# Shorter norm chains in three stages and an earlier choice of experts in a twelve-stage kernel

## What is computed

```python
# stage 1 (L0_attn): two norms in a row, then linear attention and an MLP
x = x + _L0_attn_ref(_layernorm(x), ...)      # in it: xn = _rmsnorm(x, scale1)
# stage 10 (L3_attn): retention, a norm per head, a gate
var = jnp.mean(o * o, axis=-1, keepdims=True)
o = o * jax.lax.rsqrt(var + EPS) * gnorm_w
o = o * (g * jax.nn.sigmoid(g))
return o.reshape(B, T, H * HEAD_V) @ Wo.T
# stage 11 (L3_ffn), called with _layernorm(x)
h = _layer_norm(x, ln1_g, ln1_b)
h = _self_attention(h, wq, bq, wk, bk, wv, bv, wo, bo)
x = x + h
h = _layer_norm(x, ln2_g, ln2_b)
# _moe_ffn(h): 512 tokens, 8 experts, capacity C = 128
logits = x @ wr
probs = jax.nn.softmax(logits, axis=-1)
top1 = jnp.argmax(probs, axis=-1)
m1 = jax.nn.one_hot(top1, N_EXPERTS, dtype=x.dtype)
top2 = jnp.argmax(jnp.where(m1 > 0, -jnp.inf, logits), axis=-1)
loc1 = jnp.cumsum(m1, axis=0) - 1.0
loc2 = jnp.cumsum(m2, axis=0) - 1.0 + m1.sum(0, keepdims=True)
# tokens with loc < C go to their experts' buffers; the two outputs
# are added with the renormalized probabilities as weights
```

## Time and profile before

| | |
|---|---|
| runs | 1654.95, 1656.37, 1659.03 us; median 1656.37 |
| the profiled execution: time, span | 1656.19 us, 1654.4 us |
| mean granted clock of TensorE | 0.961 |
| PE busy | 1525.7 us, 92% |
| DVE busy | 799.6 us, 48% |
| ACT busy | 621.1 us, 38% |
| POOL busy | 145.1 us, 9% |

### The profile page before, as it was taken

One profiled execution on the slowest core, in us unless ns is written; L12 is line 12 of the kernel. 1 busy time (PEld: TensorE's weight loads), 2 busy tenths in 40 slices (PEclk: granted clock), 3 DMA queues, 4 the chain that ended last, 5 costly groups with the idle time before them and its releaser, 6 DMA issues.

```text
span 1654.4 us, 23522 instructions
## 1 busy us (share of the span) xinstructions
PE 1525.7 (92%) x9628; PEld 934.4 (56%) x9628; DVE 799.6 (48%) x1418; ACT 621.1 (38%) x1161; POOL 145.1 (9%) x185
## 2 busy tenths in 40 slices
PE   7999899999999999999989899999999989677798
PEld 3667544445667554667555455555555555444697
DVE  5553530003433433332452577788889844665432
ACT  1212421011433322433521357677777782104111
POOL 0001120000000301000110312202200000000000
PEclk9999999999999999999999999999999999678699
DMA  9024133200024301022141476454956205100050
GB/s 374 30 102 165 62 110 102 74 28 27 0 102 155 121 0 34 1 102 111 35 136 80 83 144 115 99 93 86 213 84 163 37 2 217 51 1 1 1 204 13
DMA packets 40402, 147.08 MB, mean 89 GB/s; under 512 B 6092, under 2 KB 21708, under 8 KB 30668
## 3 DMA queue, kind: packets, MB, share of 16 engines
q1 hardware_dynamic: 40296, 145.58, 31.0%
HBM read 122.99 MB, written 22.56 MB: 88 GB/s over the span
## 4 chain that ended last, share of the span: by engine, by line
PE 85%; DVE 9%; ACT 4%; issue 2%; DMA 0%; SPq 0%; DVEq 0%; ACTq 0%
PE PS L156 54%; PE PS L1818 8%; PE PS L1735 7%; PE PS L1720 4%; PE PS L565 3%; PE PS L1194 2%; DVE SM L1834 1%; PE PS L1371 1%; PE PS L1204 1%; ACT CN L1417 1%; PE PS L2287 1%; PE PS L2223 1%; DVE SM L2319 1%; ACT L260 1%; PE PS L1809 1%
## 5 line engine op out<-in xcount | busy, mean ns | idle before, releaser
L1834 DVE TENSOR_REDUCE SM<-PS 128x1 f32<-128x1024 f32 x256 | 303.6, 1219 | 66.6 <-PE PS L1720 64.5
L156 PE MATMUL PS<-CT,HT 128*128 128x512 f32 x416 | 190.4, 593 | 2.0 <-ACT HT L669 2.0
L156 PE MATMUL PS<-CN,AR 128*128 128x256 f32 (+1 forms) x832 | 188.0, 371 | 0.0
L156 PEld LDWEIGHTS PS<-CN,AR 128*128 128x128 f32 x832 | 151.2, 190 | 43.9 <-issue 28.7
L156 PE MATMUL PS<-HT,AR 128*128 128x512 f32 x328 | 160.1, 641 | 15.7 <-ACT HT L330 10.4
L1735 PE MATMUL PS<-AR 49*128 49x256 bf16 (+1 forms) x1216 | 162.8, 272 | 1.1 <-DVE AR L1855 0.7
L156 PE MATMUL PS<-AR 128*128 128x512 f32 (+3 forms) x472 | 145.8, 463 | 7.0 <-DVE AR L600 2.5
L1735 PE MATMUL PS<-AR,CT 49*128 49x256 bf16 (+1 forms) x832 | 124.9, 273 | 0.6 <-DVE SM L1878 0.5
L156 PEld LDWEIGHTS PS<-AR 128*128 128x128 f32 x472 | 83.7, 192 | 69.3 <-issue 51.8
L156 PEld LDWEIGHTS PS<-HT,AR 128*128 128x128 f32 x328 | 64.8, 205 | 102.0 <-issue 99.1
L156 PEld LDWEIGHTS PS<-CT,HT 128*128 128x128 f32 x416 | 73.7, 190 | 70.9 <-issue 66.0
(11 more groups left out here) (305 smaller groups left out, 2020.0 us busy)
## 6 DMA issues: line engine op xcount, KB each, us to landing
CN<-ctx_n SPq DMA_DIRECT2D x24, 1024.0 KB, 4.8
AR<-k_parts SPq DMA_DIRECT2D x114, 128.0 KB
CT<-pack SPq DMA_DIRECT2D x7, 2048.0 KB, 7.5
k_parts<-CN SPq DMA_DIRECT2D x32, 384.0 KB, 3.7
CT<-k_parts SPq DMA_DIRECT2D x78, 128.0 KB
CN<-v_ones SPq DMA_DIRECT2D x8, 1152.0 KB, 8.9
CT<-ctx_t SPq DMA_DIRECT2D x8, 1024.0 KB, 19.0
AR<-pack SPq DMA_DIRECT2D x16, 512.0 KB, 3.9
```

The costliest lines, as they stand in the source:

```text
L156: last = te.matmul(o, l, r, start=first and k == 0, stop=final and k == n - 1, skip_group_check=True)
L1834: ve.tensor_reduce(MX9[:, p % 2, e, g % 8 // 4, g % 4:g % 4 + 1], PS[:, b:b + 2, :].rearrange("p a b -> p (a b)"), AX, ALU.max).then_inc(* ...
```

## The change

Names in the rows below: L is the line in the kernel that the row is of (the new kernel's lines are shifted).

Stage 1. Z is made from X in one norm: since the variance of H is v / (v + eps), the two scales together are 1 / sqrt(256 v), with the factor 16 staying where it was. Z, its turns and HT come first; H is made after them, for POOL only. The squares, their sums and one of the chains are gone.

```diff
-        def norm_dve(dv, s, src, dst, mv, rs, *points, name="h"):
+        def norm_dve(dv, s, src, dst, mv, rs, *points, name="h", scale=1.0, eps=1e-5):
             ve = dv.e
             dv.wait_ge(*points)
-            ve.tensor_scalar(rs, mv[:, :, 1], 1.0, 1e-5, ALU.mult, ALU.add).then_inc(*dv.inc("norm", name + "_var", s))
+            ve.tensor_scalar(rs, mv[:, :, 1], scale, eps, ALU.mult, ALU.add).then_inc(*dv.inc("norm", name + "_var", s))
...
-            norm_dve(dv, 1, X, H, xmv, s1_rs[0], *x_norm(1))
-            rms_dve(dv, 1, "z", H, Z1, s1_ss[0], s1_rs[1])
+
+            norm_dve(dv, 1, X, Z1, xmv, s1_rs[1], *x_norm(1), name="z", scale=256.0, eps=0.0)
...
             scaled("zt", W1["s1"])
+            norm_dve(dv, 1, X, H, xmv, s1_rs[0])
...
-            begin_act(ac, 1, s1_rs[0])
-            rms_act(ac, 1, "z", H, Y1, s1_ss[0], s1_rs[1], *[[p] for p in h_all(1)])
+            begin_act(ac, 1, s1_rs[1], "z")
+            norm_act(ac, 1, s1_rs[0])
...
+            out_row(0)
+            out_row(1)
+            out_row(2)
+            inverse(0)
+            out_row(3)
+            inverse(1)
+            gated(0)
+            inverse(2)
+            gated(1)
+            inverse(3)
+            gated(2)
+            gated(3)
+            turned_out_10(dv, 0)
...
+            def root(i):
+                ac.wait_ge(("o_inv", i))
+                ae.activation(rr10[:, i, :], rr10[:, i, :], ACT.Sqrt).then_inc(*ac.inc("root", "o_rs", i))
+
             for i in range(4):
                 for h in range(4):
                     ac.wait_ge(("oo", i), ("rot", 3), ("osq", i - 1, 3) if i else None)
                     ae.activation((tA, tB)[i % 2][:, tok(h)], OO[:, i, tok(h)], ACT.Square,
                                   accum_out=ss10[:, i, h:h + 1]).then_inc(*ac.inc("square", "osq", i, h))
-                ac.wait_ge(("o_inv", i))
-                ae.activation(rr10[:, i, :], rr10[:, i, :], ACT.Sqrt).then_inc(*ac.inc("root", "o_rs", i))
+                if i:
+                    root(i - 1)
+            root(3)
+            turned_out_10(ac, 1)
...
+                pl.wait_ge(("g", 10, i), ("w", 10))
+                pl.wait_last()
+                pl.e.tensor_tensor(g, g, W10["gn"].unsqueeze(1).to_broadcast([128, 4, 128]), ALU.mult).then_inc(
+                    *pl.inc("row", "gn", i))
...
+        M12 = AR[:, o + 1664:o + 1696].bitcast(BF16).rearrange("p (a b) -> p a b", b=8)
+        TRIU11, ONES11 = AR[:, o + 1696:o + 1760].bitcast(BF16), AR[:, o + 1760:o + 1824].bitcast(BF16)
+        oh11, oh11b = M12[:, 0:4, :], M12[:, 4:8, :]
...
             yield "dispatch", 0
+            yield "weights", 0
             for e in range(8):
                 yield "hidden", e
-                if e:
+                if e == 0:
+                    yield "rows", 0
+                    yield "gates", 0
+                else:
                     yield "combine", e - 1
                 if e + 1 < 8:
                     yield "dispatch", e + 1
+                    yield "gates", e + 1
                 yield "result", e
...
-            pe.wait_ge(*before, ("m1", 11), ("m2", 11))
-            te.matmul(blocks, CS["triu"], M12, start=True, stop=False, skip_group_check=True)
+            pe.wait_ge(*before, ("oh", 11), ("oh2", 11), ("counts", 11))
+            te.matmul(blocks, TRIU11, M12, start=True, stop=False, skip_group_check=True)
             for n in range(7):
                 first = n + 1 if n < 3 else 4 if n == 3 else n + 1
                 row = M12[:, n:n + 1, :].to_broadcast([128, 8 - first, 8])
-                z = te.matmul(blocks[:, first:8, :], CS["ones"], row, start=False, stop=n == 6, skip_group_check=True)
+                z = te.matmul(blocks[:, first:8, :], ONES11, row, start=False, stop=n == 6, skip_group_check=True)
...
+                if what == "rows":
+                    rows8_pe(pe, 11, GG11)
+                    pe.wait_ge(("rt", 11), ("x2", 3))
+                    for i in range(4):
+                        te.matmul(ACC[i], GT11[:, tok(i)], W11["b2"][0:8, :], start=i % 2 == 0, stop=False,
+                                  skip_group_check=True).then_inc(*pe.inc("expert", "acc_b", i))
...
+                if what == "gates":
                     b, before = PB.take(("gdt", e), ("gdt", e))
                     pe.wait_ge(*before, ("gd", e, 3))
...
-            norm_dve(dv, 11, X, X1, xmv, s11_rs[0], *x_norm(11), name="x1")
-            for i in range(4):
-                stats_dve(dv, 11, X1, st11, mv11, i, "x1", ("x1", 11, i))
-            norm_dve(dv, 11, X1, H, mv11, s11_rs[1], ("x1_mv", 11, 3))
+
+            r1, r2 = s11_rs[0], s11_rs[1]
+            dv.wait_ge(*x_norm(11))
+            ve.tensor_scalar(r1, xmv[:, :, 1], 1.0, 1e-5, ALU.mult, ALU.add).then_inc(*dv.inc("norm", "v_eps", 11))
+            dv.wait_ge(("v_eps", 11))
+            ve.reciprocal(r1, r1).then_inc(*dv.inc("norm", "v_inv", 11))
+            dv.wait_ge(("v_inv", 11))
+            ve.tensor_tensor(r2, xmv[:, :, 1], r1, ALU.mult).then_inc(*dv.inc("norm", "x1_var", 11))
+            dv.wait_ge(("x1_var", 11))
+            ve.tensor_scalar(r2, r2, 1.0, 1e-5, ALU.mult, ALU.add).then_inc(*dv.inc("norm", "x1_eps", 11))
+            dv.wait_ge(("x1_eps", 11))
+            ve.reciprocal(r2, r2).then_inc(*dv.inc("norm", "x1_inv", 11))
+            dv.wait_ge(("x1_inv", 11))
+            ve.tensor_tensor(r2, r2, r1, ALU.mult).then_inc(*dv.inc("norm", "h_inv", 11))
+            for i in range(4):
+                dv.wait_ge(("h_rs", 11))
+                ve.tensor_scalar(H[:, i, :], X[:, i, :], xmv[:, i, 0:1], r2[:, i:i + 1], ALU.subtract, ALU.mult).then_inc(
+                    *dv.inc("norm", "h", 11, i))
...
-                ve.tensor_tensor(H[:, i, :], H[:, i, :], W11["g2"], ALU.mult).then_inc(*dv.inc("norm", "hg", i))
-                dv.wait_ge(("hg", i))
-                ve.tensor_tensor(H[:, i, :], H[:, i, :], W11["b2n"], ALU.add).then_inc(*dv.inc("norm", "hb", "11b", i))
-            turn_out(dv, "11b", "ht", HT, 0)
+
+            norm_dve(dv, "11b", X2, H, mv11b, s11_rs[2], ("x2_mv", 11, 3), name="h11")
+            for i in (0, 2):
+                for kt in range(2):
+                    dv.wait_ge(("ht_ps", "11b", i))
+                    ve.tensor_scalar(HT[:, kt, tok(i)], bank("ht", "11b", i)[:, tok(kt)], W11["g2"][:, kt:kt + 1],
+                                     W11["b2n"][:, kt:kt + 1], ALU.mult, ALU.add).then_inc(*dv.inc("turn", "ht", "11b", i))
...
+            ve.tensor_reduce(mxl11, lg11, AX, ALU.max).then_inc(*dv.inc("route", "oh_top", 11))
+            first_of("oh", lg11, mxl11, eq11, m11, oh11)
+            dv.wait_ge(("oh", 11))
+            ve.scalar_tensor_tensor(out=l11, in0=oh11, scalar=-3e38, in1=lg11, op0=ALU.mult, op1=ALU.add).then_inc(
+                *dv.inc("route", "lg2", 11))
+            dv.wait_ge(("lg2", 11))
+            ve.tensor_reduce(top11b, l11, AX, ALU.max).then_inc(*dv.inc("route", "oh2_top", 11))
+            first_of("oh2", l11, top11b, eq11b, m11b, oh11b)
...
-            first_of_max_dve(dv, 11, "oh", pr11, top11, eq11, m11, oh11, ("pr", 11))
-            dv.wait_ge(("oh", 11))
-            ve.tensor_scalar(l11, oh11, -3e38, None, ALU.mult).then_inc(*dv.inc("route", "out", 11))
-            dv.wait_ge(("out", 11))
-            ve.tensor_tensor(l11, l11, lg11, ALU.add).then_inc(*dv.inc("route", "lg2", 11))
-            first_of_max_dve(dv, 11, "oh2", l11, top11b, eq11b, m11b, oh11b, ("lg2", 11))
-            ve.tensor_copy(M12[:, 0:4, :], oh11).then_inc(*dv.inc("route", "m1", 11))
-            dv.wait_ge(("oh2", 11))
-            ve.tensor_copy(M12[:, 4:8, :], oh11b).then_inc(*dv.inc("route", "m2", 11))
...
-                    ac.wait_ge(("bt_ps", e), ("hh_ps", e - 2, 1) if e > 1 else ("y_ps", 11, 3))
-                    ae.copy(BT11[p], bank("bt", e)[:, 0:256].rearrange("p (k s) -> p k s", k=2)).then_inc(
-                        *ac.inc("expert", "bt", e))
+                    for kt in range(2):
+                        ac.wait_ge(("bt_ps", e), ("hh_ps", e - 2, 1) if e > 1 else ("y_ps", 11, 3))
+                        ae.activation(BT11[p][:, kt, :], bank("bt", e)[:, tok(kt)], ACT.Identity,
+                                      scale=W11["g2"][:, kt:kt + 1], bias=W11["b2n"][:, kt:kt + 1]).then_inc(
+                            *ac.inc("expert", "bt", e))
```

117 lines of the change are left out of this document (66 added, 51 removed).

## The result

The changed kernel took 1632.46, 1637.05 and 1638.83 us (a fourth took 1817.25 at a mean granted clock of 0.828, for a reason that is not known, and is left out of every comparison); the kernel before, with one more execution beside these, 1654.95 to 1659.05. The ratio is 0.987, with a 95% interval of 0.984 to 0.990, so the change is faster by 1.3% (1.0 to 1.6%). The profiled execution took 1637.05 and spans 1635.3, against 1654.4 before: 19.1 us less, where the sum had 17.4.

What follows compares the result with a forecast made beforehand. TensorE's own work was taken as 85% of the span, with gains where it waits behind small DVE and ACT chains. Gains less the first expert's losses gave 17.4 us, from 1656.2 to 1638.8 us, range 1632.5 to 1645.

Steps and rivals of the forecast that it cites:

- stage 1, PE's wait for Z: Start of stage 1: side jobs cover the single norm, so the turns of Z follow at once; 3.4 us gained.
- stage 1, q at full rate: The eight q matmuls of stage 1 no longer run at half clock; 2.9 us gained, lower bound 0.
- stage 10, last copy of o to y: Gated output: squares a tile ahead, gn products on POOL, 1.57 us a tile on DVE; 3.6 us gained.
- stage 10, y at its start: Half rate at which the y matmuls begin: left as it was, PE being mostly empty before it; 0 gained.
- first norm of stage 11: Chain from the last statistics to H cut to six small instructions and the root; 3.5 us gained.
- projections behind it: Projections after the first norm of stage 11: clock falls and rises as before; 0 gained.
- second norm: Stage 11: g2 and b2n become columns riding on the copies of the turned tiles; 3.0 us gained (2.7 to 3.1).
- choice and counting: Stage 11: experts chosen from logits, 1.9 us gained; counts in bf16 with the softmax beside them, 2.6 us gained.
- first expert, read to dispatch 1: Stage 11, DVE's read of the counts to dispatch 1: 16.8 us becomes 17.8 through a new wait; 1.0 us lost.
- clock at expert 1: Clock falls behind that wait; some 5 us of dispatch 1, result 0, hidden 1 at half rate; 2.5 us lost.
- 3.0 if POOL's fills hold up the normalizations: Lower bound for the first norm of stage 11: 3.0 us gained if POOL's three fills and two casts delay it.
- if hidden 0 isn't mostly at half rate: Sign of a wrong forecast at the first expert, where hidden 0 was taken at half rate for about 5 us, 6.1 in all.

Runs made afterwards that it cites:

- only_s1: The kernel before with the stage 1 part alone (Z from X in one norm): median 1654.2 us, ratio 0.9943 to the kernel before.
- old_order: The changed kernel with the first expert's old order (weights, rows, b2 matmuls, then dispatch 0 with its gates): median 1639.2 us, ratio 0.983 to 0.988 to before.
- dense: The changed kernel with dispatch 1 directly behind hidden 0, rows and gates after it, b2 matmuls behind result 0: median 1631.8 us, ratio 0.978 to 0.984 to before.
- dense2: dense plus dispatch 1 ahead of hidden 0, gate products early, softmax's last steps behind D, POOL's fill and casts behind H: median 1633.1 us.
- gn_dve: The changed kernel with stage 10's four products of g with gn back on DVE: median 1643.2 us, ratio 0.987 to 0.993 to before.
- only_s10: The kernel before with the stage 10 part alone (interleaved order, gn products on POOL, copies split with ACT): median 1655.6 us, ratio 0.9959.

## Why the prediction came out as it did

The time, 1637.1 in the median of the three executions compared against 1638.8 forecast, is closer than the steps are. By step:

| Step | Forecast | Measured |
|---|---|---|
| stage 1, PE's wait for Z | 3.4 | 3.6 |
| stage 1, q at full rate | 2.9 | 3.0 |
| stage 10, last copy of o to y | 3.6 | 4.5 |
| stage 10, y at its start | 0 | 0.9 |
| first norm of stage 11 | 3.5 | 3.1 |
| projections behind it | 0 | 0.6 |
| second norm | 3.0 | 2.9 |
| choice and counting | 4.5 | 4.5 |
| first expert, read to dispatch 1 | -1.0 | +1.4 |
| clock at expert 1 | -2.5 | -1.6 |
| stages 4 and 0, untouched | 0 | -4.2 |

**Right.** Stage 1: the jobs covered the one norm that is left, and the clock stayed up, as only_s1 shows for the part alone. The choice from logits, and the counts with the softmax as the last to end. The second norm to 0.1. The new wait of PE for the copy and D, 1.8 forecast, was 1.56, and the clock fell behind it; old_order and dense have neither. Inside "choice and counting" one size was wrong and covered: the bf16 counts, forecast at 1.0 us, took 0.46 (dense2), but the softmax beside them held the read back to 0.83.

**Stage 10, mis-sized.** The step took 1.57 us a tile for inverse and gating, by adding recorded durations. The tiles came every 1.34, and the first gating started 0.9 us behind the start of the last copy instead of 1.2. DVE's timeline in the changed kernel says why:
```profile
1407.02 0.16 DVE L2103 TENSOR_SCALAR SM<-SM 128x4 f32<-128x4 f32 x1
1407.22 0.18 DVE L2105 RECIPROCAL SM<-SM 128x4 f32<-128x4 f32 x1
1407.31 1.12 DVE L2110 SCALAR_TENSOR_TENSOR CN<-CN,SM 128x128 f32<-128x128 f32 x4
```
The gating before was recorded from 1405.97 for 1.14, to 1407.11, but the inverse, which doesn't depend on it, starts at 1407.02; and the next gating starts at 1407.31, while L2105 is still on record until 1407.40, since that tile's own inverse had been made before (L2105 at 1405.88). Independent neighbours overlap by some 0.1 us; dependent ones, in the kernel before, did not. And the y matmuls spent less of themselves at half rate, 0.9 us that I had left at nothing on the ground that PE is mostly empty ahead of them in both kernels. From their start to the last X add it is 9.3 to 9.5 us in the two profiles with 11.3 us from the last copy of o to y, 9.1 in gn_dve with 8.6 us, and 7.9 to 8.6 in the nine with 6.8 us: the shorter the thin stretch ahead, the less is lost, with 0.7 us of scatter. The 0.6 of the projections can't be put down to a shorter gap: in only_s10, with the old gap of 6.7 us, the 32 matmuls took 15.95, in the kernel before 16.74 and in the changed one 16.14.

**The first norm, 0.4 short.** L2342 took 0.51 where its like take 0.17. The timeline of POOL and DVE in the changed kernel:
```profile
1422.12 0.52 POOL L2533 MEMSET CN<- 128x512 f32 x1
1422.15 0.51 DVE L2342 TENSOR_SCALAR SM<-SM 128x4 f32<-128x4 f32 x1
```
and of DVE in dense2, where POOL's fill waits for H:
```profile
1423.86 0.17 DVE L2349 TENSOR_SCALAR SM<-SM 128x4 f32<-128x4 f32 x1
```
With the fill out of the way it took 0.17 and the norm 0.34 less. The bound "3.0 if POOL's fills hold up the normalizations" had the cause and the size, and the sum went by the other end.

The Trainium skill, "SBUF — State Buffer", section "SBUF: two separate sides", has this as an exclusive lock: whichever starts first of a GpSimd instruction and a DVE instruction of certain kinds keeps the shared ports for its whole length. The trace agrees: POOL's fill starts 0.03 us ahead, and DVE's instruction ends 0.02 us behind the fill's end (0.02 to 0.03 in all seven profiles in which the fill meets it).

**The first expert, the step that failed.** The forecast had hidden 0 at half rate for some 5 us, 6.1 in all. The clock was up by 1534, while dispatch 0 was still running, and hidden 0 took 3.84. The forecast had let half rate begin anew with hidden 0, as after other gaps, though only 0.9 us of waiting stood between the two. So this step gained 1.4 instead of losing 1.0, an error of 2.4 us, of which hidden 0 is 2.3. The prediction had named it itself as a sign of being wrong, "if hidden 0 isn't mostly at half rate": by that sign it was wrong here, and only the total came out. It had the right shape otherwise: the same wait, at the same place. **Its clock term** was 0.9 too large, because the half rate was over with dispatch 1, ahead of result 0 and hidden 1.

These 3.3 us, 1.9 net in the other steps of stages 10 and 11 and 0.3 in stage 1 stood on one side, and on the other the 4.2 us of stages 0 and 4, for which the trace of the kernel before had no sign. That the sum came within 2 us is luck to this extent: without the 4.2 it would have been some 6 us off.

## What to carry to other kernels

Where PE waits behind a chain of small DVE and ACT instructions, shorten the chain by algebra (one norm for two, choice ahead of softmax), by columns instead of rows, and by moving independent work to an idle engine, and read each part's gain in its own stretch: from a fixed instruction ahead of the edit to a fixed one behind it. Lay the order of a short prologue out so that no wait stands between two groups of matmuls, even at the price of a somewhat later start (old_order: dispatch 1 0.7 us later, the first combine 0.9 earlier): the waits of 0.77 and 1.56 us cost another 1.6 by the clock, and dense got all of it back. Put POOL's fills where DVE isn't in a chain of small steps.
